# Six folding products of the cross attention weights moved from full slots 26 to 31 to fill slots 3 to 8, into the PSUM bank of the decays

## The chip, the cores and the metric

The kernel runs on one core of one Trainium2 chip. The metric is the device time of one execution in microseconds (us), the median of three runs. A core has five engines that run their own instruction streams in order and meet at semaphores: TensorE (PE in the profile, its weight loads PEld), VectorE (DVE), ScalarE (ACT), GpSimd (POOL) and SyncE (SP), which here issues nearly all DMAs.

## What is computed

A decoder layer on 32 sequences of 64 tokens, width 256, in float32. Cut to what matters:

```python
x = _layernorm(x + delta_attention(x))             # 8 heads of 128, two keys and values per token,
                                                   # short convolutions, gated delta rule over time
x = _layernorm(x + cross_attention(x, ctx, itok))  # 16 heads, keys and values from a latent of 64
x = _layernorm(x + ffn(x))                         # 256 -> 1024 -> 256, dequantized weights

# in cross_attention:
kv_c = kv @ W_kvc;  q_c = q @ W_dq
q_nope = q_c @ W_uq;  k_nope = kv_c @ W_uk;  k_rope = kv_c @ W_kr
v = kv_c @ W_uv
out = (softmax(q_nope k_nope + rope(q_c @ W_qr) rope(k_rope)) v) @ W_o
```

Two pairs of weights of the cross attention can be multiplied once, ahead of the tokens: W_uq with W_uk (the kernel calls the product w_qn) and W_uv with W_o (w_uvo). These are the "folding products" of this change: two of kind QN (8 heads each) and four of kind UVO (4 heads each).

## The kernel before

The first phase is the delta attention. Its work is cut into U = 32 units (4 groups of 8 sequences times 8 heads), and a hand-written loop over slots s = 0 to 42 pipelines them. Unit u has its keys and queries projected and convolved (K0, K1, Q) in slot u. Its decays and its gram matrices come in slot u + 1. Its values (V0, V1), gate (G), triangular solve and output come LAG = 9 slots later. So slots 1 to 8 are *fill* slots, with only the first half of the work; slots 10 to 31 are *full* slots, with both halves; after slot 31 the pipeline drains, and the tile phase (cross attention and FFN, 16 tiles of 128 tokens) begins to overlap. Each engine has its own copy of the slot loop with its own order written out, and semaphores count units.

Twenty-two preparation steps for the cross attention are threaded through the slots, one per slot, by `prepare_at(s)`. Before the change they take slots 10 to 31: sixteen steps for the latent keys (KV, TOKENS, KR, KRS for each of four groups, slots 10 to 25), then QN in slots 26 and 27 and UVO in slots 28 to 31. A folding step consists of:

- SP, two loads into the one shared input buffer `prepare_in` (L328 and L329 for QN, 384 and 256 KB; L331 and L332 for UVO, 128 and 512 KB). They are issued at the end of SP's turn for the slot before the step;
- PE, 8 or 4 matmul pairs into a PSUM bank (L518 or L521), after waiting for these loads;
- ACT, a copy from PSUM to `prepare_out` (L835);
- SP, a store of `prepare_out` to a DRAM scratch (L350 or L354), in its turn for the slot of the step.

What matters for the order is SP's queue. In its turn for slot s it issues, in this order: the keys' weights of unit s + 1 (L445, 390 KB, needed by PE at the very start of slot s + 1), from slot 8 on the values' weights (L449), four diagonal blocks of the gram of unit s - 1 (L362), in slot 2 five constants (L474), then the store of this slot's step, then the loads of the next slot's step:

```python
def load_diagonal(u):
    ...
    e.wait_ge(s_gm, 4 * u + 3)      # three of the four DVE products of unit u are done
...
    now, then = prepare_at(s), prepare_at(s + 1)
    if now is not None and now[1] != KRS:
        prepare_store(*now)
    if then is not None:
        wait(e, s_pmm, then[0])
        prepare_load(*then[1:])
```

PE in a fill slot s does: the decays product of unit s - 1 (L559, into bank EB, named decays), projections K0, K1 and Q of unit s (L528; Q goes to bank OB, named out), then the two halves of the gram of unit s - 1 (L543). DVE convolves K0, K1, Q (L1114, nine instructions), then multiplies the gram with the decays (L1127, L1133, four instructions), which is what SP's diagonal loads wait for. The first triangular solve needs the diagonals of units 0 to 3; DVE loads it in slot 5 (L1139) and POOL eliminates (L1328, L1331) from then on. In a full slot PE has its folding product between projections K0 and K1, and `output(ud)` later waits for ACT's copy, since both use bank OB; after `output`, POOL adds squares into o_sum (L1435) and PE's `norm` (L721) at the slot's end waits for that.

Of the kernel before, what the change touches and what calls it, by code (L numbers as in the profile page):

```python
# [8 lines left out]
ACT = mybir.ActivationFunctionType  # L9
# [3 lines left out]
B, S, D = 32, 64, 256  # L13
# [108 lines left out]
LAG = 9  # L122
# [16 lines left out]
def delta_phase(nc, a, st, banks, room, scratch):  # L139
    if True:  # L140
# [157 lines left out]
        def wait(e, s, n):  # L298
            if n > 0:
                e.wait_ge(s, n)  # L300

        by_rows = lambda u: u < U - LAG - 1
        PREPARE = LAG + 1
        KV, TOKENS, KR, KRS, QN, UVO = range(6)

        def prepare_at(s):
            i = s - PREPARE
            if 0 <= i < 4 * NG:
                return i, (KV, TOKENS, KR, KRS)[i % 4], i // 4
            if 4 * NG <= i < 4 * NG + 2:  # L310
                return i, QN, i - 4 * NG
            if 4 * NG + 2 <= i < 4 * NG + 6:
                return i, UVO, i - 4 * NG - 2
            return None

        ctx = pin[:, 0:KD * GT].rearrange("p (k n) -> p k n", k=KD)
# [5 lines left out]
        if True:  # L322
# [173 lines left out]

            def tensor(e, ahead):
                def prepare(s, i, kind, n):
                    if i == 0:
                        e.wait_ge(d_pconst, 80)  # L500
                    if kind == KV:
                        e.wait_ge(d_pin, 16 * (n + 1))
                    elif kind in (QN, UVO):
                        e.wait_ge(d_pin, 16 * (NG + 2 * (i - 4 * NG + 1)))
                    elif kind == TOKENS:
                        e.wait_ge(s_pout, i)
                    wait(e, s_og, s - LAG - 1)
                    if kind == KV:
                        for k in range(KD):
                            mm = e.matmul(OB[:], w_kvc2[:, k, :], ctx[:, k, :], start=(k == 0), stop=(k == KD - 1))  # L510
                    elif kind == TOKENS:
                        for j in range(4):
                            mm = e.transpose(OB[:, j * KVC:(j + 1) * KVC], kvs[0:64, j * TILE:(j + 1) * TILE], ident[0:64, 0:64])
                    elif kind in (KR, KRS):
                        mm = e.matmul(OB[:], w_kr[kind - KR][:], kvs[0:64, :], start=True, stop=True)
                    elif kind == QN:
                        for h in range(8):
                            mm = e.matmul(OB[0:QC, h * KVC:(h + 1) * KVC], half_uq[:, h, :], half_uk[:, h, :], start=True, stop=True)  # L518
                    else:
                        for h in range(4):  # L520
                            mm = e.matmul(OB[64 * (h % 2):64 * (h % 2) + 64, h // 2 * D:(h // 2 + 1) * D], some_uv[:, h, :],  # L521
                                          some_wo[:, h, :], start=True, stop=True)
                    mm.then_inc(s_pmm, 1)

                def project(c, u):
                    g, w = group(u), weights(c, u)
                    for k in range(KD):
                        mm = e.matmul(bank(c, u)[:], w[:, (k * 3 + c % 3) * 128:(k * 3 + c % 3 + 1) * 128],  # L528
                                      xT[g][:, k, :], start=(k == 0), stop=(k == KD - 1))
                    mm.then_inc(s_proj[c], 1)  # L530
# [24 lines left out]
                def decays(u):  # L555
                    e.wait_ge(s_steps, u + 1)
                    wait(e, s_ee, u)
                    wait(e, s_whiout, u - LAG + 1)
                    e.matmul(EB[:], between_l[:], flat(steps), start=True, stop=True).then_inc(s_between, 1)  # L559

# [30 lines left out]
                for s in range(1, LAG):  # L591
                    ua, ub = s, s - 1
                    e.wait_ge(d_wa[ua % 2], 16 * (ua // 2 + 1))
                    if s > 1:
                        decays(ub)
                    e.wait_ge(s_conv[K0], 3 * ua)
                    project(K0, ua)
                    e.wait_ge(s_conv[K1], 3 * ua)
                    project(K1, ua)
                    if s == 1:  # L600
                        e.wait_ge(s_z, 2)
                        e.wait_ge(s_beta, 2)
                        decays(ub)
                    e.wait_ge(s_conv[Q], 3 * ua)
                    project(Q, ua)
                    e.wait_ge(s_silu[Q], ub + 1)
                    wait(e, s_gm, 4 * ub - 2)
                    if ub == 0:
                        e.wait_ge(s_beta, 1)
                        e.wait_ge(s_twice, NG)  # L610
                    gram(0, ub)
                    wait(e, s_gm, 4 * ub)
                    if ub == 0:
                        e.wait_ge(s_beta, NG)
                    gram(1, ub)
# [204 lines left out]
            def scalar(e, ahead):  # L820
                def prepare_copy(i, kind, n):
                    if kind == KV:
                        e.wait_ge(s_pmm, i + 1)
                        wait(e, d_kv, 32 * n)
                        e.activation(kvs[:], OB[:], ACT.Copy).then_inc(s_pout, 1)
                    elif kind == TOKENS:
                        e.wait_ge(s_pmm, i + 1)
                        wait(e, s_padd, n)
                        e.activation(t2[:, 0:4 * KVC], OB[:, 0:4 * KVC], ACT.Copy).then_inc(s_pout, 1)
                    elif kind in (QN, UVO):  # L830
                        e.wait_ge(s_pmm, i + 1)
                        e.wait_ge(s_padd, NG)
                        e.wait_ge(d_pout, 16 * (NG + i - 4 * NG))
                        some = slice(0, QC) if kind == QN else slice(0, 128)
                        e.activation(t2[some, :], OB[some, :], ACT.Copy).then_inc(s_pout, 1)  # L835

                def tap(c, u):
                    j = AW + c % 3 * CONV + CONV - 1
                    e.wait_ge(s_proj[c], u + 1)
                    if place[c, u] >= 4:  # L840
                        before, unit = order[place[c, u] - 4]
                        e.wait_ge(s_silu[before], unit + 1)
                    e.activation(acc(c, u)[:], bank(c, u)[:].rearrange("p (b l) -> p b l", l=S), ACT.Copy,  # L843
                                 scale=weights(c, u)[:, j:j + 1]).then_inc(s_tap[c], 1)
# [7 lines left out]
                def silu(c, u, out):  # L852
                    e.wait_ge(s_conv[c], 3 * (u + 1))
                    e.activation(out, acc(c, u)[:], ACT.Silu).then_inc(s_silu[c], 1)  # L854
# [28 lines left out]
                def keys(j, u):  # L883
                    return KQ[u % 2][:, :, S:].rearrange("p b (l j) -> p b l j", j=NH)[:, :, :, j]
# [33 lines left out]
                for s in range(1, LAG):  # L918
                    ua, ub, h = s, s - 1, solve_at(s, 6)
                    if s > 1:  # L920
                        e.preload_act_table_set(LN_EXP)
                        exp_between(ub)
                        if s == 2:
                            e.wait_ge(s_beta, NG)
                            e.activation(beta, beta, ACT.Exp, scale=-1.0).then_inc(s_eb, 1)
                        if h is not None:
                            k_norms(h)
                        tap(K0, ua)
                        tap(K1, ua)
                        silu(Q, ub, KQ[ub % 2][:, :, 0:S])  # L930
                    else:
                        tap(K1, ua)
                    wait(e, s_gram, 2 * (ua - 1))
                    silu(K0, ua, keys(0, ua))
                    tap(Q, ua)
                    silu(K1, ua, keys(1, ua))
                    square_q(ub)

# [118 lines left out]
            def vector(e, ahead):  # L1057
                def prepare_rope(i, kind, n):
                    if kind in (KR, KRS):
                        e.wait_ge(s_pmm, i + 1)  # L1060
                        if kind == KR:
                            wait(e, d_rope, 32 * n)
                        else:
                            e.wait_ge(d_pout, 16 * (n + 1))
                        e.tensor_tensor((t1, t2)[kind - KR][:].rearrange("p (b l) -> p b l", l=S),
                                        OB[:].rearrange("p (b l) -> p b l", l=S),
                                        table[kind - KR][:, None, :].broadcast_to([128, GB, S]), ALU.mult).then_inc(s_pout, 1)
# [967 lines left out]
```

## Time and profile before

| | |
|---|---|
| three runs | 1187.59 us median (1184.17 to 1188.15) |
| the profiled execution, its own time | 1185.69 us |
| its span in the profile | 1183.9 us |
| busy: PE / PEld / DVE / ACT / POOL | 1118.0 / 772.8 / 819.6 / 704.7 / 517.7 us |
| granted TensorE clock, mean | 0.987 of full |
| start of slots 3, 4, 5 and 9 on PE (decays, L559) | 42.80, 54.05, 63.66, 108.15 us |
| `output` (L552, 32 matmuls): in full slots, and at 634.14 us | 1.15 and 1.98 us |
| start of slots 26, 27, 28, 31, 32 on PE | 476.20, 497.42, 518.64, 582.30, 603.35 us |

A slot's start is read as the start of the decays product of the unit before (L559), PE's first large product of a slot. All times of the trace are counted from the span's start; the execution's own time is 1.8 us more than the span. A bracket behind a row of the timeline gives idle time of that engine just before the row and what ended it. In the view of busy time by stretch the columns are the stretch, its length, the busy us of PE, PEld, DVE, ACT and POOL with their instruction counts, then the granted clock, the DMA engines' busy share and GB/s.

### The profile page before, as it was taken

How to read it: one execution, taken by the hardware profiler on the slowest of the kernel's cores; microseconds unless marked ns; L12 is line 12 of the kernel's file. 1: busy time of each engine (PE TensorE's matmuls, PEld its weight loads, DVE VectorE, ACT ScalarE, POOL GpSimd, SP SyncE). 2: the span in 40 equal slices, each digit the busy share in tenths (PEclk: the TensorE clock that was granted, in tenths of full speed). 3: DMA queues.
4: the chain of work that ended last, by engine and by line, in shares of the span. 5: the costliest groups of instructions: out<-in, count | busy, mean ns of one | idle time of the engine just before them, and what ended most of it. 6: DMA issues, size and time to landing. Idle time of an engine off the chain costs nothing.

```text
span 1183.9 us, 28721 instructions
## 1 busy us (share of the span) xinstructions
PE 1118.0 (94%) x11460; PEld 772.8 (65%) x11460; DVE 819.6 (69%) x1447; ACT 704.7 (60%) x1214; POOL 517.7 (44%) x717
## 2 busy tenths in 40 slices
PE   8887899999999999999998899879999999999997
PEld 3444455555555555555555566668999899989976
DVE  5997778868868778779776655666556666565552
ACT  5776567777676776776766766534443444444443
POOL 1659486585784883983976712241100000010000
PEclk9999899999999999999998999989999999999999
DMA  4223234555545454565645542331222211112100
GB/s 122 49 51 81 69 51 79 87 106 74 115 79 92 95 78 89 113 123 116 127 75 167 160 129 64 113 102 46 50 51 52 68 52 46 46 45 51 30 16 9
DMA packets 147284, 93.74 MB, mean 79 GB/s; under 512 B 80688, under 2 KB 130736, under 8 KB 146256
## 3 DMA queue, kind: packets, MB, share of 16 engines
q1 hardware_dynamic: 146000, 91.71, 35.2%
q8 instruction: 91, 1.49, 0.5%
q14 instruction: 41, 0.34, 0.1%
q10 hardware_dynamic: 1152, 0.21, 0.1%
HBM read 54.77 MB, written 14.55 MB: 59 GB/s over the span
## 4 chain that ended last, share of the span: by engine, by line
PE 74%; DVE 9%; POOL 7%; ACT 4%; issue 3%; SPq 1%; DMA 1%; ACTq 0%; DVEq 0%; POOLq 0%
PE proj L528 21%; PE out L1632 5%; PE turned_v_chain L1632 5%; PE gram L543 5%; PE turned_v_chain L1701 4%; PE proj L1691 4%; PE proj L1571 4%; DVE conv L1114 3%; POOL inverse L1331 3%; PE gram L1606 2%; POOL rank_one L1328 2%; PE out L552 2%; PE turned_v_chain L534 2%; PE decays L559 2%; PE turned_v_chain L677 1%
## 5 line engine op out<-in xcount | busy, mean ns | idle before, releaser
L1114 DVE SCALAR_TENSOR_TENSOR conv<-proj,kq_weights,conv 128x504 f32<-128x504 f32 (+2 forms) x261 | 189.7, 732 | 30.4 <-ACT conv L843 24.0
L528 PE MATMUL proj<-xT,vg_weights 128*128 128x512 f32 x384 | 190.9, 621 | 2.2 <-DVE conv L1114 2.0
L1930 POOL TENSOR_TENSOR rope<-rope_part,rope_part 128x512 f32<-128x512 f32 x32 | 40.0, 1271 | 319.1 <-DVE rope_part L1871 319.1
L1114 DVE SCALAR_TENSOR_TENSOR conv<-proj,vg_weights,conv 128x504 f32<-128x504 f32 (+2 forms) x192 | 140.7, 733 | 45.2 <-ACT conv L843 40.1
L528 PE MATMUL proj<-xT,kq_weights 128*128 128x512 f32 x348 | 167.6, 608 | 0.2 <-DVE conv L1114 0.2
L1331 POOL TENSOR_TENSOR inverse<-inverse,rank_one 128x30 f32<-128x30 f32 (+14 forms) x240 | 126.5, 527 | 18.8
L1328 POOL TENSOR_TENSOR rank_one<-inverse 128x30 f32<-128x30 f32 (+14 forms) x240 | 116.8, 487 | 15.0
L528 PEld LDWEIGHTS proj<-xT,vg_weights 128*128 128x128 f32 x384 | 68.9, 193 | 66.5 <-issue 60.4
L528 PEld LDWEIGHTS proj<-xT,kq_weights 128*128 128x128 f32 x348 | 62.7, 191 | 74.8 <-issue 69.1
L843 ACT ACTIVATE conv<-proj,kq_weights 128x512 f32<-128x512 f32 x87 | 59.6, 687 | 54.6 <-PE proj L528 54.4
L1710 ACT ACTIVATE rstd<-rstd 128x1 f32<-128x1 f32 x48 | 9.7, 202 | 136.1 <-DVE rstd L1818 136.1
L543 PEld LDWEIGHTS gram<-keys_q 128*64 128x64 f32 x896 | 56.8, 136 | 51.8 <-ACT keys_q L854 33.5
L543 PE MATMUL gram<-keys_q 128*64 128x160 f32 (+2 forms) x896 | 73.4, 293 | 9.4 <-ACT keys_q L854 9.4
L854 ACT ACTIVATE keys_q<-conv 128x512 f32<-128x512 f32 x96 | 63.4, 667 | 16.9 <-DVE conv L1114 16.2
L843 ACT ACTIVATE conv<-proj,vg_weights 128x512 f32<-128x512 f32 x64 | 43.9, 685 | 41.7 <-PE proj L528 41.5
L1691 PE MATMUL proj<-t_w_uvo,ctxT 128*128 128x256 f32 x256 | 59.4, 386 | 2.7 <-ACT ctxT L1775 2.7
L1426 POOL TENSOR_TENSOR W_scaled<-W,k_norm 128x512 f32<-128x512 f32 x32 | 35.3, 1104 | 54.6 <-ACT W L947 54.6
L1701 PE MATMUL turned_v_chain<-t_w_down,hid 128*128 128x256 f32 x256 | 58.0, 379 | 0.9 <-DVE hid L1878 0.9
L1435 POOL TENSOR_TENSOR o_sum<-o_sum,q_sq 128x512 f32<-128x512 f32 x23 | 29.5, 1283 | 64.2 <-ACT o_sum L1046 64.2
L1176 DVE COPY Y<-turned_v_chain 32x256 f32<-32x256 f32 x64 | 27.1, 424 | 41.1 <-PE turned_v_chain L628 39.6
L1691 PEld LDWEIGHTS proj<-t_w_uvo,ctxT 128*128 128x128 f32 x256 | 48.5, 194 | 9.7 <-issue 3.5
L1701 PEld LDWEIGHTS turned_v_chain<-t_w_down,hid 128*128 128x128 f32 x256 | 48.6, 190 | 7.7 <-DVE hid L1878 1.1
(257 smaller groups left out, 2487.6 us busy)
## 6 DMA issues: line engine op xcount, KB each, us to landing
kq_weights<-in_kq_w SPq DMA_DIRECT2D x32, 390.0 KB, 6.5
vg_weights<-in_vg_w SPq DMA_DIRECT2D x32, 390.0 KB, 6.2
o_scratch<-oT SPq DMA_DIRECT2D x32, 256.0 KB, 2.2
o_in<-o_scratch SPq DMA_DIRECT2D x16, 512.0 KB, 4.0
o_rs<-o_rs_quarters SPq DMA_DIRECT2D x88, 64.0 KB, 6.1
diagonal<-gram_decayed SPq DMA_DIRECT2D x128, 32.0 KB, 1.9
inverse<-inverse SPq DMA_DIRECT2D x32, 128.0 KB, 2.8
q_first<-rope SPq DMA_DIRECT2D x128, 32.0 KB, 1.9
```

Source lines behind the costliest of these rows:

```text
L528: mm = e.matmul(bank(c, u)[:], w[:, (k * 3 + c % 3) * 128:(k * 3 + c % 3 + 1) * 128], xT[g][:, k, :], start=(k == 0), stop=(k == KD - 1))
L543: mm = e.matmul(out[p, b % 4, cols], kq[:, b, S:][:, p], kq[:, b, cols], start=True, stop=True)
L843: e.activation(acc(c, u)[:], bank(c, u)[:].rearrange("p (b l) -> p b l", l=S), ACT.Copy, scale=weights(c, u)[:, j:j + 1]).then_inc(s_tap[c ...
L854: e.activation(out, acc(c, u)[:], ACT.Silu).then_inc(s_silu[c], 1)
L1114: e.scalar_tensor_tensor(acc(c, u)[:, :, back:], src[:, :, 0:S - back], weights(c, u)[:, j:j + 1], acc(c, u)[:, :, back:], ALU.mult, ALU.a ...
L1328: e.tensor_tensor(product, X[:, k + 1:, k:k + 1].broadcast_to([128, n, k]), X[:, k:k + 1, 0:k].broadcast_to([128, n, k]), ALU.mult).then_i ...
L1331: e.tensor_tensor(X[:, k + 1:, 0:k], X[:, k + 1:, 0:k], product, ALU.add).then_inc(s_elim, 1)
L1571: mm = e.matmul(out_bank(u)[:, 0:D], o_in[u % 2][:, h, :], w_out[:, h, :], start=(h == 0), stop=(h == H - 1))
L1632: mm = e.matmul(ffn_bank[r][:, (2 * i + j) * TILE:(2 * i + j + 1) * TILE], wt[:, k, (2 * r + j) * 128:(2 * r + j + 1) * 128], x2T[:, k, :] ...
L1691: mm = e.matmul(b0[:, 0:D], ctxT[:, hp].rearrange("p b q -> p (b q)"), w_uvo[:, hp, :], start=(hp == 0), stop=(hp == XH // 2 - 1))
L1701: mm = e.matmul(b6[:, 0:D], hid[:, k, :], w_down[:, k, :], start=(k == 0), stop=(k == FJ - 1))
L1930: e.tensor_tensor(turned[half][:].rearrange("p b r q -> p r b q"), parts[2 * half][:], parts[2 * half + 1][:], op).then_inc(s_turned, 1)
```

## The change

The six folding steps take slots 3 to 8 (FOLD = LAG - 6), as steps 0 to 5; the sixteen steps of the latent keys keep slots 10 to 25 and become steps 6 to 21; slots 26 to 31 have no step. In a fill slot PE's folding product comes after projection Q and ahead of the gram, and it is written to EB, the bank of the decays, after ACT's exponential of that slot has read the bank; the next decays product waits for ACT's copy. ACT's copy comes after the tap of Q. The loads and the store keep their place in SP's turn, so the loads of step s are issued in the turn for slot s - 1, from slot 2 on. Counts in the waits change with the new numbering.

```diff
-        PREPARE = LAG + 1
+        PREPARE, FOLD = LAG + 1, LAG - 6
         def prepare_at(s):
+            if FOLD <= s < FOLD + 6:
+                return s - FOLD, (QN if s < FOLD + 2 else UVO), (s - FOLD if s < FOLD + 2 else s - FOLD - 2)
             i = s - PREPARE
             if 0 <= i < 4 * NG:
-                return i, (KV, TOKENS, KR, KRS)[i % 4], i // 4
-            if 4 * NG <= i < 4 * NG + 2:
-                return i, QN, i - 4 * NG
-            if 4 * NG + 2 <= i < 4 * NG + 6:
-                return i, UVO, i - 4 * NG - 2
+                return 6 + i, (KV, TOKENS, KR, KRS)[i % 4], i // 4
             return None
...
             def tensor(e, ahead):
                 def prepare(s, i, kind, n):
...
                     elif kind in (QN, UVO):
-                        e.wait_ge(d_pin, 16 * (NG + 2 * (i - 4 * NG + 1)))
+                        e.wait_ge(d_pin, 32 * (i + 1))
...
-                    wait(e, s_og, s - LAG - 1)
+                    if kind in (QN, UVO):
+                        e.wait_ge(s_ee, s)
+                    else:
+                        wait(e, s_og, s - LAG - 1)
...
-                            mm = e.matmul(OB[0:QC, h * KVC:(h + 1) * KVC], half_uq[:, h, :], half_uk[:, h, :], start=True, stop=True)
+                            mm = e.matmul(EB[0:QC, h * KVC:(h + 1) * KVC], half_uq[:, h, :], half_uk[:, h, :], start=True, stop=True)
...
                 def decays(u):
                     e.wait_ge(s_steps, u + 1)
                     wait(e, s_ee, u)
+                    if u < LAG and prepare_at(u) is not None:
+                        e.wait_ge(s_pout, prepare_at(u)[0] + 1)
...
                     e.wait_ge(s_conv[Q], 3 * ua)
                     project(Q, ua)
+                    if prepare_at(s) is not None:
+                        prepare(s, *prepare_at(s))
                     e.wait_ge(s_silu[Q], ub + 1)
...
                     elif kind in (QN, UVO):
                         e.wait_ge(s_pmm, i + 1)
-                        e.wait_ge(s_padd, NG)
-                        e.wait_ge(d_pout, 16 * (NG + i - 4 * NG))
+                        wait(e, d_pout, 16 * i)
                         some = slice(0, QC) if kind == QN else slice(0, 128)
-                        e.activation(t2[some, :], OB[some, :], ACT.Copy).then_inc(s_pout, 1)
+                        e.activation(t2[some, :], EB[some, :], ACT.Copy).then_inc(s_pout, 1)
...
                     silu(K0, ua, keys(0, ua))
                     tap(Q, ua)
+                    if prepare_at(s) is not None:
+                        prepare_copy(*prepare_at(s))
                     silu(K1, ua, keys(1, ua))
```

## Rows read from the trace of the kernel before

**Rows 1.** The page's chain that ended last, shares of the span by engine.
```profile
PE 74%; DVE 9%; POOL 7%; ACT 4%; issue 3%; SPq 1%; DMA 1%; ACTq 0%; DVEq 0%; POOLq 0%
```

**Rows 2.** Busy time by stretch: slots 4 and 26.
```profile
54.05:63.66 9.61, 8.60 (x47) 4.68 (x47) 7.63 (x13) 6.85 (x11) 2.67 (x3) 1.00 0.25 57
...
476.20:497.42 21.22, 21.22 (x255) 12.85 (x250) 14.93 (x24) 15.52 (x29) 19.49 (x31) 1.00 0.60 121
```

**Rows 3.** The chain in order of time, slots 26 and 28: start, us, what.
```profile
484.92 1.91 PE proj L528 x4
...
489.94 1.24 PE gram L543 x15
...
492.88 3.63 PE proj L528 x8
...
527.36 1.91 PE proj L528 x4
...
532.20 1.24 PE gram L543 x15
```

**Rows 4.** Timeline of POOL, slots 25 to 31.
```profile
475.60 1.91 POOL L1396 TENSOR_TENSOR inverse<-inverse,rho 128x1024 f32<-128x1024 f32 x1 [0.70 <-DVE inverse L1154]
...
494.97 1.28 POOL L1435 TENSOR_TENSOR o_sum<-o_sum,q_sq 128x512 f32<-128x512 f32 x1
...
514.82 1.27 POOL L1435 TENSOR_TENSOR o_sum<-o_sum,q_sq 128x512 f32<-128x512 f32 x1 [1.86 <-ACT o_sum L1046]
...
592.47 1.04 POOL L1426 TENSOR_TENSOR W_scaled<-W,k_norm 128x512 f32<-128x512 f32 x1 [0.62 <-ACT W L947]
...
599.53 1.28 POOL L1435 TENSOR_TENSOR o_sum<-o_sum,q_sq 128x512 f32<-128x512 f32 x1 [2.07 <-ACT o_sum L1046]
```

**Rows 5.** Timeline of PE at the end of slot 26.
```profile
496.44 0.43 PE L721 MATMUL turned_v_chain<-o_sum,ones_mean 128*32 128x128 f32 x8
```

**Rows 6.** Timeline of DVE in slot 28, behind the folding product.
```profile
532.96 0.74 DVE L1114 SCALAR_TENSOR_TENSOR conv<-proj,kq_weights,conv 128x504 f32<-128x504 f32 x1 [0.66 <-ACT conv L843]
...
534.11 0.41 DVE L1191 TENSOR_TENSOR kq_decayed<-kq_decayed,turned_v_chain 64x256 f32<-64x256 f32 x1 [0.41 <-PE turned_v_chain L677]
```

**Rows 7.** Timeline of SP's queue in the fill.
```profile
50.53 0.43 SPq L445 DMA_DIRECT2D kq_weights<-in_kq_w  x1
...
79.71 2.54 SPq L362 DMA_DIRECT2D diagonal<-gram_decayed  x4
```

**Rows 8.** Timeline of SP's queue at a folding step, slot 28.
```profile
520.49 0.60 SPq L350 DMA_DIRECT2D w_qn_scratch<-prepare_out  x1
...
521.61 0.46 SPq L332 DMA_DIRECT2D prepare_in<-in_xwo  x1
```

**Rows 9.** Issue to landing of the second load of a step: QN (L329, two), UVO (L332, four).
```profile
DMA to landing us min/median/max: 4.2/4.2/4.3
...
DMA to landing us min/median/max: 4.2/4.9/6.0
```

**Rows 10.** Timeline of PE in the fill and at slot 9.
```profile
61.33 1.17 PE L543 MATMUL gram<-keys_q 128*64 128x128 f32 x15 [1.00 <-ACT keys_q L854]
...
108.15 1.13 PE L559 MATMUL decays<-steps,between_lhs 128*128 128x512 f32 x2 [2.19 <-POOL steps L1371]
109.11 5.29 PE L528 MATMUL proj<-xT,vg_weights 128*128 128x512 f32 x8
```

**Rows 11.** Timeline of DVE in slots 4 and 5.
```profile
65.57 0.68 DVE L1127 TENSOR_TENSOR gram_decayed<-turned_v_chain,decayed 128x512 f32<-128x512 f32 x1
...
67.26 2.27 DVE L1114 SCALAR_TENSOR_TENSOR conv<-proj,kq_weights,conv 128x504 f32<-128x504 f32 x3 [0.68 <-ACT conv L843]
...
70.16 2.19 DVE L1139 STREAM_TRANSPOSE inverse<-diagonal 128x512 f32<-128x512 f32 x2 [0.63 <-DMA diagonal<-gram_decayed]
```

**Rows 12.** Timeline of PE at two idle stretches, slots 6 and 33.
```profile
82.57 1.17 PE L543 MATMUL gram<-keys_q 128*64 128x128 f32 x15 [2.44 <-ACT keys_q L854]
...
634.14 1.98 PE L552 MATMUL out<-W_scaled,V 128*64 128x64 f32 x32 [5.18 <-POOL W_scaled L1426]
```

More of the change, by code:

```diff
@@ L498, in prepare @@
                 def prepare(s, i, kind, n):
-                    if i == 0:
-                        e.wait_ge(d_pconst, 80)
                     if kind == KV:
-                        e.wait_ge(d_pin, 16 * (n + 1))
+                        if n == 0:
+                            e.wait_ge(d_pconst, 80)
+                        e.wait_ge(d_pin, 16 * (12 + n + 1))
                     elif kind in (QN, UVO):
-                        e.wait_ge(d_pin, 16 * (NG + 2 * (i - 4 * NG + 1)))
+                        e.wait_ge(d_pin, 32 * (i + 1))
                     elif kind == TOKENS:
                         e.wait_ge(s_pout, i)
-                    wait(e, s_og, s - LAG - 1)
+                    if kind in (QN, UVO):
+                        e.wait_ge(s_ee, s)
+                    else:
+                        wait(e, s_og, s - LAG - 1)
                     if kind == KV:
@@ L517, in prepare @@
                         for h in range(8):
-                            mm = e.matmul(OB[0:QC, h * KVC:(h + 1) * KVC], half_uq[:, h, :], half_uk[:, h, :], start=True, stop=True)
+                            mm = e.matmul(EB[0:QC, h * KVC:(h + 1) * KVC], half_uq[:, h, :], half_uk[:, h, :], start=True, stop=True)
                     else:
                         for h in range(4):
-                            mm = e.matmul(OB[64 * (h % 2):64 * (h % 2) + 64, h // 2 * D:(h // 2 + 1) * D], some_uv[:, h, :],
+                            mm = e.matmul(EB[64 * (h % 2):64 * (h % 2) + 64, h // 2 * D:(h // 2 + 1) * D], some_uv[:, h, :],
                                           some_wo[:, h, :], start=True, stop=True)
@@ L828, in prepare_copy @@
                         wait(e, s_padd, n)
+                        if n == 0:
+                            e.wait_ge(d_pout, 16 * 6)
                         e.activation(t2[:, 0:4 * KVC], OB[:, 0:4 * KVC], ACT.Copy).then_inc(s_pout, 1)
@@ L1063, in prepare_rope @@
                         else:
-                            e.wait_ge(d_pout, 16 * (n + 1))
+                            e.wait_ge(d_pout, 16 * (6 + n + 1))
                         e.tensor_tensor((t1, t2)[kind - KR][:].rearrange("p (b l) -> p b l", l=S),
```

## The prediction

> **What bounds the kernel now.** I read the page's chain that ended last first: 74% of the span is PE [rows 1], so a product taken off PE can be worth its full length, if nothing else is close behind. Then the busy time by slot [rows 2]: in full slot 26 PE is busy 21.22 of 21.22 us, with POOL close at 19.49. In fill slot 4 PE is busy 8.60 of 9.61 us, and the idle 1.00 us stands just ahead of the gram [rows 10], exactly where the folding product is to go. By this view the fill has room for most of a product and the full slots have none. The view that decides is a third one, SP's queue in the fill: not whether PE has time for the product, but when its operands are there.
>
> **What leaves the full slots.** A product costs more than its own row, since the next product also starts without overlap. From projection K0 to the gram it is 489.94 - 484.92 = 5.02 us with a QN product between, 532.20 - 527.36 = 4.84 with UVO, and 3.63 for two projections back to back [rows 3]. So QN is worth 1.39 and UVO 1.21 us: 2 x 1.39 + 4 x 1.21 = 7.6 us if PE stays the bound in all six slots. Slot by slot, what is late next:
>
> - Slot 26: POOL has no idle from 475.60 to its o_sum at 494.97, which ends at 496.25; PE's norm, which needs it, starts at 496.44 [rows 4, 5]. POOL's run began with DVE's part of slot 25 and doesn't move. Allowing 0.05 us from POOL to PE, the slot gains 0.14, not 1.39.
> - Slot 27: POOL then sits idle 1.86 us waiting for ACT's squares [rows 4]; 0.14 + 1.39 fit in it. Gain 1.39.
> - Slot 28: DVE runs from the sum's subtraction through the solve's transposes into slot 29 without a break; ahead of it stand 0.66 + 0.41 = 1.07 us of idle that the earlier K1 and sum can use [rows 6]. Gain 1.07.
> - Slots 29 to 31: 1.21 each. For the last two, 2.42 in all, the drain of slot 32 hangs on POOL, which has 0.62 + 2.07 us of idle to give [rows 4].
>
> Sum 0.14 + 1.39 + 1.07 + 3.63 = 6.2 us. The bounds are 0 (POOL or DVE closes up everywhere; they carry 19.49 and 14.93 of 21.22) and 7.6. ACT's copies, six stores and twelve loads also leave these slots; SP and ACT have idle there, so that is worth nothing.
>
> **What the fill slots get.** The product itself: 1.39 or 1.21 against 1.00 us of idle would cost 0.4 or 0.2 a slot. ACT's copy (0.6 us, the form of L835) moves K1's silu, not the gram of that slot, which needs Q's; ACT is busy 6.85 of 9.61 us [rows 2]. Counted at nothing.
>
> The loads are another matter. SP issues the loads of step s + 1 behind the four diagonal loads of unit s - 1, and these wait for DVE's third product of the gram of unit s - 1. That gram now stands on PE behind step s's product. So the six steps form a loop, product, gram, DVE, diagonals, store, load, next product, and none of it overlaps. In full slots the same order hides the load, since PE comes to the product half a slot later. Its length, counted from a slot's start:
>
> - the second gram half ends 0.1 us in, DVE's product takes 0.68 [rows 11], diagonals start at 0.85;
> - four diagonals 2.54, with the gap 2.6 [rows 7]; from the store's start to the second load's 1.12 [rows 8];
> - landing 4.2 to 6.0; four of the six took 4.2 or 4.3 [rows 9]; the fill's DMA share is 0.25 against 0.60 [rows 2], so I take 4.3;
> - sum: operands land 8.87 us into the slot. PE wants them at 61.33 - 1.00 - 54.05 = 6.28 [rows 2, 10], the third projection's end. It waits 2.6 us;
> - product 1.21, then 2.33 from the gram's start to the next slot (61.33 to 63.66). The slot takes 12.4 us (12.6 with QN).
>
> Behind PE's wait are queued the gram, and through it DVE, the diagonals and the first solve. Now the walk. Step 0's loads are issued when SP is done with the constants, at 50.53, where the weights for slot 4 were [rows 7]: second load near 51.1, landing 55.4, against 42.80 + 6.28 = 49.1: 6.3 us of wait. The weights follow at 51.7 and land in front of slot 4, which starts at 55.4 + 1.39 + 2.33 = 59.1. Slot 5 at 59.1 + 12.6 = 71.7, slot 6 at 84.1. In slot 5 DVE has the solve: K0's convolution ended 67.26 + 2.27 - 63.66 = 5.87 into the slot, now 77.6; the solve starts there instead of 70.16 and the diagonals of unit 4 follow 79.71 - 70.16 = 9.55 later [rows 7, 11], at 87.1. Then 2.6 + 1.12 + 4.3 + 1.21 + 2.33 brings slot 7 to 98.7, slot 8 to 111.1, slot 9 to 123.5. Before, slot 9 began at 108.15: **+15.4 us**. That old start had waited 2.19 us for POOL [rows 10]; POOL's chain starts with the solve and is 7.4 us later, so it is no longer what slot 9 waits for. With landings of 6.0 in each step it is 15.4 + 6 x 1.7 = 25.6; with landings such that PE never waits, 0 to 1.6 (the products beyond the idle 1.00).
>
> The Trainium skill, "DMA: Bandwidth & Descriptors", section "Anatomy of one DMA", gives a transfer some 2.0 us plus bytes over 436 GB/s. Its fit is for the other issuing path. An estimate from it for the pair of 640 KB is 3.5 us from the first issue, about 3.0 from the second; by that the walk would be 6 x 1.3 = 7.8 us shorter, and the result still slower than before. The same page's "Rules for kernel authors" says to issue a DMA early, compute, and wait late; this step is issued late and waited for early.
>
> **The clock.** At slot 9, after 2.19 us of idle, two projections took 5.29 instead of 3.63 us [rows 3, 10], which is half clock for a part of it: 1.7 us. After 5.18 us of idle L552 took 1.98 instead of 1.15; after 2.44 us the gram at 82.57 ran at its usual 1.17 [rows 12]. So the waits of 6.3 us (slot 3) and about 4.7 us (slot 6) should each bring such a fall onto the product and gram: 2 x 1.7 = 3.4 us. The four waits of 2.6 us lie where rows show both; I put them at one fall in four, 1.7, and take off the 1.7 of slot 9, whose wait is gone. Bounds: -1.7 and 6 x 1.7 = 10.2.
>
> The Trainium skill, "TensorE: Matmul & The Clock Gate", section "HAM oscillation", describes just this: groups of matmuls with waits for a DMA between them, each group run at the lower clock. [...]
>
> **Sum.** +15.4 + 3.4 - 6.2 = +12.6 us. On the profiled execution's own 1185.69 that is 1198.3 (span 1196.5); it lies 1.9 under the median of the three runs, 1187.59, to which I add it: **1200.2 us**.
>
> **The rivals.**
> 1. *Loads in time, faster.* If the loads landed within 6.28 us of the slot's start, the fill would cost 0 to 1.6 us and the full slots give 6.2: 1181.4 to 1183.0. For it: PE idle and a quiet DMA in the fill. Against it: 0.85 + 2.6 + 1.12 are spent before the second load is out, and no second load landed under 4.2. It turns when the wait per slot is under about 1 us, that is a landing under 2.7. Chance 0.09.
> 2. *Late, but light.* No fall of the clock, full 7.6 from the full slots, 1.7 of slot 9 saved: 15.4 - 1.7 - 7.6 = +6.1, 1193.7. Chance 0.15, with what lies between it and the forecast's own range.
> 3. *Late and heavy.* Landings of 5.5 to 6.0 because the weights now follow right behind, or a fall of the clock in each slot: +15.4 + 7 to 10 - 6.2 = +16 to +19 for either, 1204 to 1207; both at once 1215. Chance 0.17.
> 4. *Full slots give nothing*, as POOL or DVE close up: +18.8, 1206.4. Chance 0.05.
> 5. *A wash*, the loop half hidden by something that I don't see: within 0.3%. Chance 0.03.
>
> The forecast keeps 0.51, with 1197 to 1204 as its own range. For 8 in 10 it reaches to the light case and well into the heavy: 1193 to 1210. 0.3% is 3.6 us, about what a measurement of this kernel tells from none. Faster 0.09, same 0.03, slower 0.88.
>
> **What would show it.** In the changed kernel's timeline PE is idle ahead of L518 and L521 in slots 3 to 8, ended by the DMA into prepare_in, 6, 2.6, 2.6, 4.7, 2.6 and 2.6 us, some 21 in all; the loads start within 5 us of each slot's start; slot 9 starts near 123 to 127; the granted clock of 54 to 60 and 95 to 100 is below 1. Slot 26 stays at about 21.1 us and slots 27 and 29 to 31 fall to about 19.8 to 20.4. If PE shows no wait for prepare_in and slot 9 starts under 112, the loop is not there and the forecast is wrong in sign.

## The result: 1.58% slower, and the profile after

The changed kernel takes 1205.25 us (median of six runs, 1202.88 to 1206.04) against 1185.48 (median of six, 1183.56 to 1188.15) for the one before: a ratio of 1.0158 [1.0142, 1.0173], some 19 us slower. The forecast was 1200.2 in 1193 to 1210. The sign and the range hold; the difference was forecast as 12.6 us and is 19.8 by the medians, and 2.1 us of that gap do not show in the 1200.2 because it was added to a median of 1187.59. I compare the profiled executions from here on: spans 1204.2 and 1183.9.

The page's chain that ended last. PE has less of it than in [rows 1], while DVE, POOL and the DMAs have more:

```profile
PE 69%; DVE 11%; POOL 8%; issue 4%; ACT 3%; SPq 2%; DMA 2%; ACTq 0%; POOLq 0%; DVEq 0%
```

Busy time by stretch of the kernel after: the fill from slot 3 to slot 9's start, then slots 26 and 27. Columns: stretch, its length, busy time (instructions) of PE, PEld, DVE, ACT, POOL, granted clock, DMA share, GB/s.

```profile
42.66:133.87 91.21, 70.27 (x340) 43.88 (x340) 58.10 (x96) 49.07 (x69) 50.10 (x77) 0.85 0.34 99
500.08:521.13 21.05, 19.97 (x240) 11.49 (x234) 14.77 (x24) 15.38 (x29) 19.32 (x31) 1.00 0.56 90
521.13:540.97 19.84, 19.84 (x241) 11.50 (x235) 14.77 (x24) 14.34 (x24) 18.20 (x27) 1.00 0.49 81
```

The reader is to see the first row's length and clock. The same stretch before ran from 42.80 to slot 9's start at 108.15 [rows 10], 65.35 us. It is now 91.21, PE is idle for 21 of them, and the mean granted clock is 0.85: for about a third of the stretch PE had the lower of its two levels (1.2 GHz, not 2.4). From 54.40 to 61.00, behind the first wait, it had nothing else: the granted clock there is 0.50. In slot 26 [rows 2] PE is no longer busy throughout, but POOL is at 19.32 of 21.05, so the slot kept its length.

The timeline of PE in the fill, kernel after. Columns: start, us, engine, line, operation, tiles, shape, count, and in brackets the idle time before and what ended it.

```profile
54.44 2.82 PE L519 MATMUL decays<-prepare_in 128*96 128x64 f32 x16 [5.50 <-DMA prepare_in<-in_ukT]
57.19 2.14 PE L544 MATMUL gram<-keys_q 128*64 128x128 f32 x15
...
61.37 1.13 PE L562 MATMUL decays<-steps,between_lhs 128*128 128x512 f32 x2
...
70.69 2.35 PE L519 MATMUL decays<-prepare_in 128*96 128x64 f32 x16 [3.04 <-DMA prepare_in<-in_ukT]
...
85.05 1.97 PE L522 MATMUL decays<-prepare_in 128*64 128x256 f32 x8 [2.66 <-DMA prepare_in<-in_xwo]
...
100.15 1.98 PE L522 MATMUL decays<-prepare_in 128*64 128x256 f32 x8 [4.04 <-DMA prepare_in<-in_xwo]
...
114.86 1.26 PE L522 MATMUL decays<-prepare_in 128*64 128x256 f32 x8 [2.69 <-DMA prepare_in<-in_xwo]
115.90 2.09 PE L544 MATMUL gram<-keys_q 128*64 128x128 f32 x15
...
129.01 1.74 PE L522 MATMUL decays<-prepare_in 128*64 128x256 f32 x8 [3.01 <-DMA prepare_in<-in_xwo]
130.53 2.09 PE L544 MATMUL gram<-keys_q 128*64 128x128 f32 x15
...
133.87 1.13 PE L562 MATMUL decays<-steps,between_lhs 128*128 128x512 f32 x2
134.84 3.60 PE L529 MATMUL proj<-xT,vg_weights 128*128 128x512 f32 x8
```

All six products wait for the second load of their step: 20.9 us in all. Behind each wait the product or the gram is longer than it should be: the first half of the gram takes 1.87 to 2.14 us where it took 1.17 [rows 10]. From the product's start to the gram's it is 2.75, 2.28, 1.76, 1.76, 1.04 and 1.52 us (the forecast had 1.39 for the first two and 1.21), from the gram's start to the next slot's 4.18, 3.14, 3.02, 3.98, 3.82 and 3.34 (forecast 2.33). Over these forecast intervals, which are from rows at full clock, that is 3.5 + 7.5 = 11.0 us. At slot 9, on the other hand, the two projections are back at 3.60 us from 5.29 [rows 10], and the wait ahead of them is gone.

SP's queue around one step, kernel after:

```profile
62.20 2.63 SPq L360 DMA_DIRECT2D diagonal<-gram_decayed  x4
64.88 0.60 SPq L348 DMA_DIRECT2D w_qn_scratch<-prepare_out  x1
65.52 0.43 SPq L326 DMA_DIRECT2D prepare_in<-in_uqT  x1
65.98 0.45 SPq L327 DMA_DIRECT2D prepare_in<-in_ukT  x1
```

This is the loop of the forecast in rows: diagonals 0.83 us into slot 4 (0.85 forecast), the second load 3.78 us behind them (3.72), and the product 70.69 - 65.98 = 4.71 us behind that. From the second load's issue to the product the six steps take 3.57, 4.71, 4.41, 4.92, 4.43 and 4.75 us, 4.5 on average, where I had taken 4.3.

Where the 20.3 us between the two spans lie:

| stretch | before | after | difference |
|---|---|---|---|
| up to slot 3 | 42.80 | 42.66 | -0.1 |
| slots 3 to 8 | 65.35 | 91.21 | +25.9 (11.0 of it the clock, 14.9 the waits and products) |
| slot 9 | 27.50 | 25.87 | -1.6 (its fall of the clock is gone) |
| slots 10 to 25 | 340.55 | 340.34 | -0.2 |
| slots 26 to 31 | 127.15 | 120.67 | -6.5 |
| behind slot 32's start | 580.55 | 583.45 | +2.9 |

The last row is not the change's doing as far as it can be told. The same stretch took 578.4, 582.9, 583.3, 583.0, 580.1, 582.1, 583.3 and 583.5 us in the profiled executions of the eight kernels below, with no relation to what was altered; the spans of the changed kernel's own six runs go from 1201.1 to 1204.2.

### The profile page after: what moved, and what is told of

Its sections match the earlier page's. It is cut to its first block, busy times and chain, and to the rows that moved or that the text cites. A ratio compares the mean times of both kernels' runs of the same rounds, so it can differ in the third digit from the quotient of the medians.

```text
span 1204.2 us, 28720 instructions
## 1 busy us (share of the span) xinstructions
PE 1129.0 (94%) x11460; PEld 785.6 (65%) x11460; DVE 819.8 (68%) x1447; ACT 705.0 (59%) x1214; POOL 517.7 (43%) x717
## 3 DMA queue, kind: packets, MB, share of 16 engines
q8 instruction: 91, 1.49, 0.5%
## 4 chain that ended last, share of the span: by engine, by line
PE 69%; DVE 11%; POOL 8%; issue 4%; ACT 3%; SPq 2%; DMA 2%; ACTq 0%; POOLq 0%; DVEq 0%
PE proj L529 17%; PE out L1640 5%; PE gram L544 5%; PE turned_v_chain L1640 5%; PE turned_v_chain L1709 4%; DVE conv L1122 4%; PE proj L1699 4%; PE proj L1579 3%; POOL inverse L1339 3%; POOL rank_one L1336 3%; PE gram L1614 2%; PE turned_v_chain L535 2%; PE out L553 2%; PE decays L562 1%; PE proj L1628 1%
## 5 line engine op out<-in xcount | busy, mean ns | idle before, releaser
L544 PEld LDWEIGHTS gram<-keys_q 128*64 128x64 f32 x896 | 62.4, 146 | 41.0 <-ACT keys_q L860 21.1
L544 PE MATMUL gram<-keys_q 128*64 128x160 f32 (+2 forms) x896 | 79.1, 309 | 2.0 <-ACT keys_q L860 2.0
L1374 POOL TENSOR_TENSOR decayed_causal<-decayed,causal 128x512 f32<-128x512 f32 x31 | 39.6, 1277 | 45.7 <-ACT decayed L872 45.4
```

Source lines behind the costliest of these rows:

```text
L544: mm = e.matmul(out[p, b % 4, cols], kq[:, b, S:][:, p], kq[:, b, cols], start=True, stop=True)
L1374: e.tensor_tensor(eem(u)[:], EE[u % 2][:], causal[:, None, :].broadcast_to([128, GB, S]), ALU.mult).then_inc(s_eem, 1)
```

## The experiments

The theory: SP issues a step's loads too late, since they stand behind the diagonals in its queue, and each wait for them brings a fall of the clock as well; the full slots gain what was forecast. Rivals: the products themselves cost it (POOL's or ACT's work in the fill, the bank of the decays); the clock falls without the waits; the full slots gain less, and the tail takes it back.

**1. The loads ahead of the diagonals.** The change stays; only SP's order is altered.

```diff
+                    early = prepare_at(s + 1)
+                    if early is not None and early[1] in (QN, UVO):
+                        wait(e, s_pmm, early[0])
+                        prepare_load(*early[1:])
                     if live(ub) and s != U:
                         load_diagonal(ub)
...
-                    if then is not None:
+                    if then is not None and then[1] not in (QN, UVO):
```

> The changed kernel, with each folding step's two loads issued ahead of the diagonals in SP's turn instead of behind the store. Theory of the loop (operands are late because their loads queue behind the diagonals, which wait for a gram that stands behind the product): the load then starts when the product before it ends, lands about 5.2 us later, and PE asks for it 2.33 + 6.28 = 8.6 us later, so PE's waits for prepare_in go from 21 us to 0 to 1, slot 9 starts near 109 to 110 instead of 133.9, and the time is 4 to 6 us under the kernel before (ratio 0.995 to 0.997). Rival (the product, ACT's copy and the shared bank of the decays are what costs): the waits only change their name, slot 9 stays later than 120 and the time stays above the kernel before.

Measured: 1177.89 us, ratio to the kernel before 0.9938 [0.9918, 0.9957]. SP's turn for slot 4 (which started at 53.05), then PE's timeline, kernel of this run:

```profile
61.06 0.43 SPq L330 DMA_DIRECT2D prepare_in<-in_xwo  x1
65.26 2.55 SPq L360 DMA_DIRECT2D diagonal<-gram_decayed  x4
```

```profile
42.12 1.12 PE L566 MATMUL decays<-steps,between_lhs 128*128 128x512 f32 x2 [1.85 <-DMA kq_weights<-in_kq_w]
...
48.23 1.49 PE L523 MATMUL decays<-prepare_in 128*96 128x64 f32 x16
...
69.12 1.08 PE L526 MATMUL decays<-prepare_in 128*64 128x256 f32 x8
...
85.88 1.13 PE L566 MATMUL decays<-steps,between_lhs 128*128 128x512 f32 x2 [1.87 <-DMA kq_weights<-in_kq_w]
86.84 5.29 PE L533 MATMUL proj<-xT,kq_weights 128*128 128x512 f32 x8
...
107.91 1.10 PE L566 MATMUL decays<-steps,between_lhs 128*128 128x512 f32 x2 [1.06 <-ACT prepare_out L845]
```

With the load issued 4.2 us ahead of the diagonals instead of 3.8 behind, no product waits. Slots 3 to 8 take 107.91 - 42.12 = 65.79 us, against 65.35 without any product in them. So the products, ACT's copies and the bank cost 0.4 us net in the fill, and nearly all of the 25.9 us was lateness and its clock. Net, because the two stretches differ in more than the products: this one has a fall of the clock in slot 7 (the projections at 5.29 us) and a wait of 1.06 us for ACT's copy out of the shared bank ahead of slot 9, the one before a wait of 2.19 us for POOL in that place [rows 10]. The gain is larger than I expected (0.9938 against 0.995 to 0.997, slot 9 at 107.91 against 109 to 110). The place of four lines on SP decides the sign of the whole change.

**2. The six steps left out.**

```diff
         def prepare_at(s):
-            if FOLD <= s < FOLD + 6:
-                return s - FOLD, (QN if s < FOLD + 2 else UVO), (s - FOLD if s < FOLD + 2 else s - FOLD - 2)
             i = s - PREPARE
...
```

The counts in the waits follow, and the two weights come unfolded from DRAM.

> The six folding steps are left out altogether (loads, products, copies, stores; the two weights come unfolded from DRAM, so the output is not the layer's). It prices the full slots alone. Theory: slots 26 to 31 give 6.5 us as in the changed kernel (0.2, 1.4, 1.2, 1.3, 1.2, 1.2), the fill is that of the kernel before (slot 9 at 108), and the whole is 6 to 7 us under the kernel before (ratio near 0.9945). Rival (the tail after slot 32, which lost 2.9 us in the changed kernel, loses them because slots 26 to 31 are shorter): the whole gains only 3 to 4 us.

Measured: 1178.68 us, ratio 0.9943 [0.9922, 0.9964]. PE's timeline:

```profile
107.27 1.56 PE L563 MATMUL decays<-steps,between_lhs 128*128 128x512 f32 x2 [2.21 <-POOL steps L1380]
...
476.07 1.12 PE L563 MATMUL decays<-steps,between_lhs 128*128 128x512 f32 x2
...
497.17 1.12 PE L563 MATMUL decays<-steps,between_lhs 128*128 128x512 f32 x2
...
517.00 1.12 PE L563 MATMUL decays<-steps,between_lhs 128*128 128x512 f32 x2
```

Slot 9 starts where it did before, with its wait for POOL. Slots 26 to 31 take 21.10, 19.83, 19.84, 20.36, 19.84 and 19.83 us, together 120.8 as in the changed kernel (120.7). The whole gain is 6.8 us by the ratio, 4.3 to 9.2 by its interval (5.9 by the medians), which leaves out the rival's 3 to 4 us, if not by much: the tail does not take the 6.5 us back. Run 1 is as fast as a kernel that doesn't compute the products at all.

**3. One step's loads instead of six.** The products of slots 4 to 8 use what lies in the buffer.

```diff
-                    if then is not None:
+                    if then is not None and not (then[1] in (QN, UVO) and then[0] > 0):
...
-                        e.wait_ge(d_pin, 32 * (i + 1))
+                        e.wait_ge(d_pin, 32)
```

> The changed kernel with the loads of the first folding step alone; the other five steps multiply the same operands again, so five of the six folded parts are wrong in value. Products, copies, stores and the shared bank stay. Loop theory: only the wait of slot 3 stays (5.5 us); slots 4 to 8 take 0.2 to 0.4 us more than in the kernel before or as much; slot 9 starts at 113 to 116 instead of 133.9, and the time is within 2 us of the kernel before. Rival (product, copy and bank are the cost): slot 9 stays near 130.

Measured: 1187.5 us, ratio 1.0018 [1.0006, 1.003]. PE's timeline:

```profile
55.19 2.83 PE L519 MATMUL decays<-prepare_in 128*96 128x64 f32 x16 [6.34 <-DMA prepare_in<-in_ukT]
...
61.76 1.12 PE L562 MATMUL decays<-steps,between_lhs 128*128 128x512 f32 x2
...
95.28 2.07 PE L562 MATMUL decays<-steps,between_lhs 128*128 128x512 f32 x2 [2.58 <-DMA kq_weights<-in_kq_w]
```

Slot 3 alone is 61.76 - 42.58 = 19.18 us long instead of 11.25, so one late load costs 7.9 us; slots 4 to 8 together are 0.8 us longer than before, though their products and copies are all there. It is the five repeated loads that make the rest of the loop. Slot 9 began at 116.69, a little later than the 113 to 116 that I had, as the keys' weights came late in slot 7 and brought a fall of their own; the time is 2.1 us over the kernel before by the ratio and 3.0 by the medians, where I had "within 2 us".

**4. The waits kept, the clock held.** PE does 5, 2, 2, 4, 2 and 2 needless matmul pairs ahead of its waits.

```diff
                     elif kind in (QN, UVO):
+                        e.wait_ge(s_ee, s)
+                        for _ in range((5, 2, 2, 4, 2, 2)[i]):
+                            e.matmul(EB[:], ident[:], xT[0][:, 0, :], start=True, stop=True)
                         e.wait_ge(d_pin, 32 * (i + 1))
```

> The changed kernel with filler matmuls of 128x512 (5, 2, 2, 4, 2, 2 in slots 3 to 8, 0.9 us each at the full clock, results overwritten) on PE while it waits for prepare_in. Loads and their lateness stay. Clock theory: products and grams behind the waits took 11 us more than at the full clock in the changed kernel; with PE kept busy the falls go, the granted clock of 43 to 125 us is 1.00, slots 4 to 8 take 12.4 to 12.8 us each, slot 9 starts at 122 to 125, and the time is 8 to 11 us under the changed kernel (ratio to the kernel before 1.006 to 1.009), less up to 1.7 us for a fall that may come back at slot 9. Rival (the products and grams are long because of the bank or of DMA traffic): they stay long and slot 9 stays at 133 to 135.

Measured: 1195.73 us, ratio 1.0085 [1.0067, 1.0103]. PE's timeline, then the busy time of the fill:

```profile
48.85 4.46 PE L504 MATMUL decays<-xT,ident 128*128 128x512 f32 x10
54.54 1.57 PE L522 MATMUL decays<-prepare_in 128*96 128x64 f32 x16 [1.23 <-DMA prepare_in<-in_ukT]
56.04 1.17 PE L547 MATMUL gram<-keys_q 128*64 128x128 f32 x15
...
124.17 1.12 PE L565 MATMUL decays<-steps,between_lhs 128*128 128x512 f32 x2
125.13 3.60 PE L532 MATMUL proj<-xT,vg_weights 128*128 128x512 f32 x8
```

```profile
42.74:124.17 81.43, 72.65 (x375) 39.69 (x375) 58.16 (x96) 48.40 (x69) 50.04 (x77) 1.00 0.38 111
```

The product in slot 3 starts at 54.54 as in the changed kernel (54.44): the load is as late as ever. But the gram is back at 1.17 us, the granted clock is 1.00, and slots 3 to 8 take 81.43 us instead of 91.21. So of the 25.9 us, 81.43 - 65.35 = 16.1 us stay at full clock as waits and products, and 9.8 us go with the falls. By the medians it is 1205.25 - 1195.73 = 9.5 us, by the two ratios 8.7. This is a little less than the falls themselves, since other things moved too: from their slot's start the six products began 2.4 us later in all than in the changed kernel, 1.1 of it in slot 6, where the diagonals came 2.51 us into the slot instead of 1.49. That is also why slots 4 to 8 (13.25, 12.80, 14.60, 12.33 and 12.83 us) are partly longer than the 12.4 to 12.8 that I expected. With this run's own intervals (1.50 and 0.91 us from product to gram, about 2.3 from there to the next slot) the falls of the changed kernel come to 12.2 us, with the forecast's to 11.0; 9.8 is what the time got back.

**5. The product behind the gram**, and ACT's copy behind the squares. The load gets more time, the loop through the gram is cut.

```diff
-                    if prepare_at(s) is not None:
-                        prepare(s, *prepare_at(s))
                     e.wait_ge(s_silu[Q], ub + 1)
...
                     gram(1, ub)
+                    if prepare_at(s) is not None:
+                        prepare(s, *prepare_at(s))
...
```

> The changed kernel with PE's folding product behind the gram instead of ahead of it, and ACT's copy behind the square of Q. SP's order is untouched, so the loads are as late as before, 8.9 us into the slot. Theory: the lateness costs because the gram, DVE and the diagonals stand behind the waiting product; behind the gram PE asks for the operands at 6.28 + 2.33 = 8.6 us, waits 0.3 to 1.0 us, and what is left is the product (1.2) and the next decays product's wait for ACT's copy (0.7). Slots 4 to 8 take 10.5 to 12 us, slot 9 starts at 113 to 118, the time is within 3 us of the kernel before. Rival (late operands cost the same wherever the product stands): slot 9 stays near 130 or later.

Measured: 1191.68 us, ratio 1.0041 [1.0016, 1.0066]. PE's timeline:

```profile
53.70 1.57 PE L519 MATMUL decays<-prepare_in 128*96 128x64 f32 x16 [2.01 <-DMA prepare_in<-in_ukT]
...
56.04 1.57 PE L562 MATMUL decays<-steps,between_lhs 128*128 128x512 f32 x2 [0.77 <-ACT prepare_out L841]
57.40 4.87 PE L529 MATMUL proj<-xT,kq_weights 128*128 128x512 f32 x8
...
118.67 1.10 PE L562 MATMUL decays<-steps,between_lhs 128*128 128x512 f32 x2 [0.78 <-ACT prepare_out L841]
```

Every wait for a load is gone but 2.01 us in slot 3. In its place the decays of the next slot wait for ACT's copy out of their bank, 0.8 us in five slots and 2.77 in one. Slot 8 takes 107.38 to 118.67, 11.3 us: 9.6, most of a product, and the copy. At the end of a slot the product has no cover, and the bank shared with the decays, for which run 1 waited in one place alone, costs in every slot here. Slots 3 to 8 take 14.03, 13.62, 13.28, 13.15, 11.29 and 11.29 us, so three of the last five lie above the 10.5 to 12 that I expected. Slots 4 and 6 have a fall of the clock in them, behind the waits of 2.01 and 2.77 us: their first two projections take 4.87 and 5.27 us instead of 3.60, about 1.7 us of each slot. Slot 9 began at 118.67 (expected 113 to 118), and the kernel is 4.9 us slower than the one before by the ratio (expected: within 3).

**6. POOL's last rope addition cut to one column**, the cover taken from POOL's chain into slot 26.

```diff
-                        e.tensor_tensor(t1[:], t1[:], t2[:], ALU.add).then_inc(s_padd, 1)
+                        cols = slice(0, GT if n < NG - 1 else 1)
+                        e.tensor_tensor(t1[:, cols], t1[:, cols], t2[:, cols], ALU.add).then_inc(s_padd, 1)
```

> The changed kernel with POOL's last rope addition (slot 25, 1.27 us) cut to one column of 512, which leaves the rope part of the last group's keys wrong. Theory: slot 26 gained only 0.2 us from losing its folding product because POOL ran without a break from slot 25 to the o_sum of slot 26; with 1.2 us less on POOL the slot falls from 21.05 to about 19.85 us and the time by 1.2 us under the changed kernel. Rival (PE or DVE held slot 26): it stays at 21.05. The whole time is too coarse to tell 1.2 us; the slot's own length decides.

Measured: 1201.71 us, ratio 1.0138 [1.012, 1.0156]. POOL's timeline in slot 26 of the changed kernel, then of this run:

```profile
504.53 1.28 POOL L1458 TENSOR_TENSOR prepare_cos<-prepare_cos,prepare_out 128x512 f32<-128x512 f32 x1
...
518.84 1.26 POOL L1443 TENSOR_TENSOR o_sum<-o_sum,q_sq 128x512 f32<-128x512 f32 x1
```

```profile
502.49 0.19 POOL L1459 TENSOR_TENSOR prepare_cos<-prepare_cos,prepare_out 128x1 f32<-128x1 f32 x1
...
515.71 1.26 POOL L1443 TENSOR_TENSOR o_sum<-o_sum,q_sq 128x512 f32<-128x512 f32 x1
```

Slot 26 starts at 500.08 and 498.02, so o_sum comes 18.76 and 17.69 us into it, and the slot takes 21.05 and 19.98 us: both fall by 1.07 (expected 1.2). POOL held slot 26, as the forecast said, and not PE. The whole time fell by more, 2.4 us by the ratios and 3.5 by the medians, and the fill of this profiled execution is 0.95 us shorter though nothing in it was altered: differences of that size in the whole time say nothing here.

**7 and 8. More for SP's order.** In run 7 the five constants of slot 2 are moved to SP's turn for slot 8, on top of run 1. In run 8, on top of both, the keys' weights of units 4 to 9 are issued ahead of the diagonals as well.

```diff
-                    if s == 2:
+                    if s == LAG - 1:
                         for tile, n in ((w_kvc2, "w_kvc2"), (w_kr[0], "w_kr"), (w_kr[1], "w_krs"),
```

```diff
...
-                    if live(ua + 1):
+                    if live(ua + 1) and not 3 <= s < LAG:
+                        keys_weights(ua + 1)
...
+                    if 3 <= s + 1 < LAG:
+                        keys_weights(ua + 2)
                     if live(ub) and s != U:
                         load_diagonal(ub)
```

> The kernel with the loads ahead, and the five constants of the preparation issued in turn 8 instead of turn 2. Theory: in turn 2 they stand 3.2 us in front of the keys' weights of slot 4, which PE waited for; the wait of 1.0 us at the start of slot 4 goes, and the gram side fills part of it: 0.5 to 1.0 us under the kernel with the loads ahead, ratio to the kernel before 0.992 to 0.994. Rival: DVE holds slot 4 anyway, no gain.

> As the one before, and the keys' weights of slots 4 to 8 are issued one place earlier too, ahead of the diagonals. In the kernel with the loads ahead PE waits for these weights 1.00 us in slot 4 and 1.87 in slot 7, and one fall of the clock (1.7 us) follows the latter. Theory: both waits go, and with them the fall: 2 to 4 us under the kernel with the loads ahead, ratio to the kernel before 0.990 to 0.992. Rival: POOL's elimination, which holds slots 6 to 9 in the kernel before, holds them here too, and the ratio stays at 0.993 to 0.994.

Measured: 1178.70 us, ratio 0.9946 [0.9928, 0.9964], and 1178.49 us, ratio 0.9949 [0.9931, 0.9968]: neither is to be told from run 1. PE's timeline of run 7, ACT's of run 8 and PE's of run 8, then ACT's of run 1:

```profile
86.20 1.12 PE L566 MATMUL decays<-steps,between_lhs 128*128 128x512 f32 x2 [2.28 <-DMA kq_weights<-in_kq_w]
...
107.15 1.12 PE L566 MATMUL decays<-steps,between_lhs 128*128 128x512 f32 x2 [1.67 <-POOL steps L1383]
```

```profile
85.98 0.60 ACT L850 ACTIVATE prepare_out<-decays 128x512 f32<-128x512 f32 x1 [2.48 <-DMA w_uvo_scratch<-prepare_out]
```

```profile
42.30 1.49 PE L571 MATMUL decays<-steps,between_lhs 128*128 128x512 f32 x2 [1.98 <-DMA kq_weights<-in_kq_w]
43.59 4.97 PE L538 MATMUL proj<-xT,kq_weights 128*128 128x512 f32 x8
```

```profile
85.05 0.60 ACT L845 ACTIVATE prepare_out<-decays 128x512 f32<-128x512 f32 x1 [2.33 <-DMA w_uvo_scratch<-prepare_out]
```

Run 7 gained 1.07 us early (slot 4 begins 9.86 us behind slot 3, in run 1 10.93). Slot 4 gave 0.68 of it back and slot 8 0.62, the latter to a wait for POOL ahead of slot 9, as in [rows 10]. Its fill is still 1.6 us shorter than run 1's (64.20 against 65.79), since the wait of 2.28 us in slot 7 brought no fall of the clock where run 1's 1.87 did; the medians do not show it. In run 8 the keys' weights are in time in slots 4 and 7. In slot 7 that frees nothing: PE's decays wait 1.92 us at 86.72 for ACT's copy, and that copy had waited 2.48 us for the landing of the store before. The same wait was there in run 1, with 2.33 us, and its copy ended at 85.65, 0.23 us ahead of the decays, so the weights had hidden it. And what run 8 gained by the weights of slot 4 (1.00 us) it lost again by a fall of the clock in slot 3, some 1.7 us, behind a wait of 1.98 us; in run 1 the same wait was 1.85 and brought none. My expectation that the keys' weights were the last thing in the way was wrong: another wait ended at nearly the same time. Run 1 has the lowest ratio of all kernels here: 0.6% faster than the kernel before, and 1 - 0.9938 / 1.0158 = 2.2% faster than the changed one.

## Why the prediction was right, and where it was off

- **The sign and the cause: right.** The loop through the gram, DVE, the diagonals and the loads is there, with waits of 5.50, 3.04, 2.66, 4.04, 2.69 and 3.01 us (20.9) where 6.3, 2.6, 2.6, 4.7, 2.6 and 2.6 (21.4) were forecast. That the sums agree so well is in part luck: a miss of 1.5 us down and one of 1.0 up nearly cancel. Runs 1 and 3 show by intervention that the position and the repetition of the loads make it.
- **The walk: +15.4 forecast, 14.9 measured** with the clock's part taken off. The first wait was shorter by 0.8 since the load landed 3.57 us after its issue, and slot 6's by 0.7; four others were longer by 0.1 to 0.4. Counting the products' own length in the fill, ACT's copy and the bank at nothing beyond the idle was right as long as the product stands ahead of the gram (run 1: 0.4 us); run 5 shows what it costs without that cover. The estimate of 3.0 us from the fit in the Trainium skill, "DMA: Bandwidth & Descriptors", section "Anatomy of one DMA", is not what these rows show: one of six came near it, at 3.57, and five took 4.41 to 4.92.
- **The full slots: -6.2 forecast, -6.5 measured.** By slot 0.17, 1.38, 1.22, 1.28, 1.21 and 1.22 us, against 0.14, 1.39, 1.07 and three times 1.21. Run 6 shows the reason for the first, POOL. Slot 28's bound by DVE was 0.15 too tight. That rival 4 might close them up is refuted, and run 2 refutes that the tail takes them back.
- **The clock: +3.4 forecast, +9.4 measured** (11.0 in slots 3 to 8, less 1.6 at slot 9; 8.2 with run 4's 9.8). This is the step that failed, in its size: "The four waits of 2.6 us lie where rows show both; I put them at one fall in four". Waits of 2.66 to 3.04 us brought a fall each time, at 1.2 to 1.7 us each (5.6 where 1.7 was put down), and those behind the two long waits cost 3.2 and 2.2, where the sum had 1.7 each. Run 4 took the falls away and left the lateness: 9.8 us came back. The forecast's own upper bound, a fall behind each of the six waits at 10.2 us, was nearer than its 3.4; the one row at 82.57 [rows 12] had been given too much weight. The Trainium skill, "TensorE: Matmul & The Clock Gate", section "HAM oscillation", describes groups of matmuls that run at the lower clock each time, behind each wait for a DMA. The trace agrees for all six groups, also for the waits of 2.66 and 2.69 us, which are shorter than those of its example.
- **What that makes of the cases.** What happened is rival 3, "late and heavy", in its form of a fall in each slot (1204 to 1207, chance 0.17), and not the forecast's own 1197 to 1204. The parts that it spoke of come to 14.9 + 9.4 - 6.5 = +17.8 us, within its +16 to +19; the stretch behind slot 32, of which it knew nothing, adds 2.9 in the profiled executions. The marks set for the trace held for the waits and the full slots; slot 9 at 123 to 127 did not, it began at 133.87.
- **Left open:** the 2.9 us behind slot 32 in the two profiled executions. They vary by as much between kernels that don't differ there, and no run here isolates them.

## What to carry to other kernels

An engine's idle time is room for work only if the operands are there by then: before work is moved into it, follow the loads through the queue that issues them, and ask what that queue waits for just ahead of them. When a move makes a loop over a queue, try the load's position first; here four lines turned +1.6% into -0.6%. Price a new wait ahead of TensorE with the slower clock behind it: here 9.8 us of clock came on top of 16.1 us of waits and products.

## What the runs showed of the hardware

- **A wait and the granted clock.** In slots 3 to 8 and at the start of slot 9 of all kernels here, every idle stretch of PE of 2.58 us or more was followed by matmuls at the lower level: 13 of 13 (the six above, 6.34 and 2.58 in run 3, 2.77 in run 5, 5.38, 3.07, 3.55 and 3.22 in run 6). Between 1.85 and 2.47 us both occur: 1.87 (run 1), 1.92 and 1.98 (run 8), 2.01 (run 5), 2.19 (before), 2.21 (run 2), 2.35 and 2.47 (run 6) with a fall; 1.85 (run 1), 1.86 and 2.28 (run 7) and 2.44 (before and run 2) without. So the length of the one wait does not decide there, and one row without a fall is weak evidence that the next will have none.
- **Nor does the length of the wait set the price of a fall.** Slot 4 of the changed kernel and of run 6 is the same program. Behind 3.04 us the product and gram took 1.7 us more than at full clock; behind 3.07 us in run 6, whose rows follow, they took 3.4.

```profile
69.14 2.82 PE L519 MATMUL decays<-prepare_in 128*96 128x64 f32 x16 [3.07 <-DMA prepare_in<-in_ukT]
71.90 2.14 PE L544 MATMUL gram<-keys_q 128*64 128x128 f32 x15
...
76.21 1.12 PE L562 MATMUL decays<-steps,between_lhs 128*128 128x512 f32 x2
```

- **A fall need not show on the first matmuls behind the wait.** In slot 7 the product behind the 2.69 us still took 1.26 us, near its 1.08 in run 1, and only the gram behind it took 2.09 instead of 1.17. Whoever looks at the waiting instruction's own row alone misses most of the price.
- **Needless matmuls in a wait keep the clock.** With them 1.15 to 1.71 us of idle were left ahead of each product, no fall followed (granted clock 1.00 in run 4), and the kernel was 9.5 us faster by the medians and 8.7 by the ratios, though no operand came sooner.
